# Mixture of experts on one core: weighted expert rows summed in DRAM by ordered, accumulating scatters

## The reference

```python
xn = layernorm(x)
x = x + segment_sum(edge_weight[:, None] * xn[dst], src, 6250) + attention(xn)   # a linear-cost attention, 8 heads
z = layernorm(x)
logits = z @ gate_w + gate_b                     # 16 experts
v, idx = top_k(logits, 2);  w = softmax(v)       # two experts per token
h = relu(z @ w1[e] + b1[e]);  o_e = h @ w2[e] + b2[e]      # 256 -> 512 -> 256, only for e in idx
y = z + sum_k w[k] * o_idx[k]
out = x + (layernorm(y) * gamma + beta)
```

## Time and profile before

| | us |
|---|---|
| median of 3 runs | 2754.63 (2744.38 to 2778.39) |
| the profiled execution | 2739.31 |
| its span, first to last instruction | 2737.4 |
| before the gate | 0 to 1913.2 |
| gate and table | 1913.2 to 2120.7 |
| expert tiles | 2120.7 to 2560.2 |
| combine | 2560.2 to 2737.4 |

### The profile page before, as it was taken

The page is one execution under the profiler, slowest core; times in us unless marked ns, Lnnn a source line. Parts: engine busy times, 40 slices in busy tenths (PEclk is TensorE's granted clock), DMA queues, the critical chain, the costliest instruction groups (busy, mean ns, idle before and its releaser), DMA issues.

```text
span 2737.4 us, 43467 instructions
## 1 busy us (share of the span) xinstructions
PE 2028.5 (74%) x12138; PEld 1334.9 (49%) x12139; DVE 1622.2 (59%) x4163; ACT 819.7 (30%) x2169; POOL 1294.0 (47%) x1239
## 2 busy tenths in 40 slices
PE   4656766888888887888888888888552999999400
PEld 3434543455444453444444444444552999999300
DVE  6888888888888885444444445444444233233377
ACT  4645631111111111222222222222321444444332
POOL 1263343777777775565655566553454000000375
PEclk9768978999999998998989898988555999999755
DMA  5300010222222222232322222247822333333343
GB/s 168 119 31 27 24 28 28 83 81 81 79 80 81 81 82 64 83 89 81 89 77 83 84 89 86 84 76 65 296 73 98 99 106 106 104 105 108 100 120 119
DMA packets 147105, 243.46 MB, mean 89 GB/s; under 512 B 27874, under 2 KB 104932, under 8 KB 146949
## 3 DMA queue, kind: packets, MB, share of 16 engines
q0 software_dynamic: 55488, 149.11, 20.2%
q1 hardware_dynamic: 88500, 89.91, 10.2%
q10 hardware_dynamic: 2960, 2.55, 0.3%
HBM read 190.08 MB, written 51.38 MB: 88 GB/s over the span
## 4 chain that ended last, share of the span: by engine, by line
PE 36%; another core or an unknown queue 7%; issue 6%; DVE 5%; POOL 3%; DMA 2%; ACT 1%; DVEq 1%; SPq 1%; ACTq 0%; POOLq 0%
PE bank L1956 8%; PE b L1716 7%; PE bqk L1976 7%; PE bank L1833 4%; PE bqk L1844 3%; PE b L1728 2%; POOL big L741 2%; DMA big<-xn_dram,big 2%; POOL big L710 1%; PE bank L1916 1%; DVE big L1466 1%; DVE acc L1259 1%; ACT mid L896 1%; DVE big L1249 1%
## 5 line engine op out<-in xcount | busy, mean ns | idle before, releaser
L710 POOL DMA_INDIRECT big<-xn_dram,big x880 | 916.1, 1041 | 529.4 <-issue 201.4
L1716 PE MATMUL b<-big 128*128 128x256 f32 x1760 | 538.4, 434 | 96.8 <-DVE acc L1259 46.2
L1716 PEld LDWEIGHTS b<-big 128*128 128x128 f32 x1760 | 338.1, 210 | 340.2 <-issue 179.8
L1259 DVE TENSOR_TENSOR acc<-acc,b 128x256 f32 x440 | 183.9, 418 | 366.6 <-remote 195.0
L741 POOL DMA_INDIRECT big<-y_dram,idxz x100 | 112.3, 1123 | 491.6 <-issue 484.0
L1249 DVE TENSOR_SCALAR big<-big 128x128 f32<-128x128 f32 x880 | 300.5, 363 | 7.8 <-DVE big L1299 7.7
L879 ACT ACTIVATE big<-bank 128x512 f32<-128x512 f32 (+1 forms) x208 | 105.4, 576 | 501.9 <-PE bank L1833 276.9
L1956 PEld LDWEIGHTS bank<-late,mid 128*128 128x128 f32 x1872 | 228.6, 193 | 7.6 <-DVE mid L1583 1.7
L1956 PE MATMUL bank<-late,mid 128*128 128x128 f32 x1872 | 229.2, 276 | 1.5 <-DVE mid L1583 1.5
L1976 PE MATMUL bqk<-big,mid 128*128 x928 | 219.5, 379 | 0.0
L1592 DVE TENSOR_TENSOR mid<-bqk,mid 128x256 f32<-128x256 f32 x116 | 49.3, 425 | 246.4 <-PE bqk L1976 246.4
(11 more groups left out here) (322 smaller groups left out, 3186.3 us busy)
## 6 DMA issues: line engine op xcount, KB each, us to landing
big<-w SPq DMA_DIRECT2D x8, 2048.0 KB
mid<-z_dram SPq DMA_DIRECT2D x120, 128.0 KB, 2.1
mid<-b SPq DMA_DIRECT2D x118, 128.0 KB, 3.0
y_dram<-mid SPq DMA_DIRECT2D x116, 128.0 KB, 1.7
big<-xn_dram,big POOLq DMA_INDIRECT x880
acc<-x_pad SPq DMA_DIRECT2D x10, 640.0 KB, 6.4
xn_dram<-big SPq DMA_DIRECT2D x10, 640.0 KB
y_out<-big SPq DMA_DIRECT2D x10, 640.0 KB
```

The lines of the kernel that those rows point to most:

```text
L710: pool.indirect_dma_start(out=gx[t % EB], out_offset=None, in_=xn_dram, in_offset=bass.IndirectOffsetOnAxis(ap=dstA[:, t:t + 1], axis=0)). ...
L1259: v.tensor_tensor(mine, mine, ps_pair[p % 2][:, 0:C], ALU.add).then_inc(s_add, 1)
L1716: a = pe.matmul(ps_pair[p % 2][:, 0:C], wd[t % (2 * EB)], gx[t % EB], start=(j == 0), stop=(j == 1))
```

## The change

The experts' results no longer go to y_dram to be gathered by token. There is a table sum_dram with one row per token. In the gate, SP stores z of each unit there. z's scattered rows are four elements wider (ZW = 260): the token's number, its first expert, the difference of its two softmax weights and the lower weight. So the row itself says where its result belongs and how it is weighted. For each expert tile DVE reads these columns (meta), adds the bias; ACT multiplies the rows by their weights (weigh); POOL scatters them with addition onto sum_dram, each scatter awaiting the one before. The combine loads plain rows, which hold z plus both weighted results. z tiles have two buffers instead of four, results four instead of two. Gate and combine loops are written out (static addresses) where they were loops of the engines. POOL adds beta to acc during the expert tiles and multiplies by gamma in the combine.

SP:

```diff
-            for a in range(0, 20, U):
-                sp.dma_start(z_dram[X * R + a * P:X * R + (a + U) * P, :].rearrange("(p r) c -> p (r c)", p=P),
-                             zero).then_inc(s_zz, 16)
+            sp.dma_start(sum_dram[NP:NP + P, :], zero[:, 0:C]).then_inc(s_zz, 16)
+            sp.dma_start(beta_b[:], beta.partition_broadcast(P)).then_inc(s_gb, 16)
...
             for e in range(0, X, 4):
                 sp.dma_start(w2s[:, e:e + 4], w2[e:e + 4].rearrange("e (c p) f -> p e c f", p=P)).then_inc(s_w, 16)
+            for u in range(NU):
+                sp.wait_ge(s_z, (u + 1) * U)
+                sp.dma_start(sum_dram[u * U * P:(u + 1) * U * P, :].rearrange("(u p) c -> p u c", p=P),
+                             zt5[u % 2][:, :, 0:C]).then_inc(s_zst[u % 2], 16)
+            sp.wait_ge(s_dz, 4)
+            sp.dma_start(z_dram[X * R:, :].rearrange("(r p) c -> p r c", p=P),
+                         padrow.unsqueeze(1).broadcast_to([P, 20, ZW])).then_inc(s_pz, 16)
...
             with sp.Fori(0, FT // 4) as i:
                 for k in range(4):
                     t = 4 * i + k
                     sp.wait_ge(f_zT, t + 1)
-                    load_z(t + 4, k)
+                    sp.wait_ge(f_meta, t + 1)
+                    load_z(t + 2, k % 2)
                     sp.wait_ge(f_yo, t + 3)
-                    sp.dma_start(y_dram[ds(t * P, P), :], yo[k % 2]).then_inc(s_yst[k % 2], 16)
                     load_b2(t + 2, k % 2)
...
+            for u in range(NU):
+                sp.dma_start(zc[u], sum_dram[u * U * P:(u + 1) * U * P, :].rearrange("(u p) c -> p u c", p=P)).then_inc(s_zl[u // 2], 16)
```

POOL:

```diff
+            for t in range(FT):
+                pool.wait_ge(f_ys, t + 1)
+                if t:
+                    pool.wait_ge(s_ysc[(t - 1) % 4], 16 * ((t - 1) // 4 + 1))
+                pool.indirect_dma_start(out=sum_dram, in_=yo[t % 4], in_offset=None,
+                                        out_offset=bass.IndirectOffsetOnAxis(ap=idxy[t % 4][:, 0:1], axis=0),
+                                        compute_op=ALU.add).then_inc(s_ysc[t % 4], 16)
+                if 4 <= t < 4 + NT:
+                    mine = acc[:, t - 4, :]
+                    pool.tensor_tensor(mine, mine, beta_b[:], ALU.add).then_inc(s_xb, 1)
+            pool.wait_ge(s_gb, 32)
+            for u in range(NU):
+                pool.wait_ge(s_fn, u + 1)
+                pool.tensor_tensor(zc[u], zc[u], gamma_b.unsqueeze(1).broadcast_to([P, U, C]), ALU.mult).then_inc(s_gm, 1)
```

ACT:

```diff
+            def gate_z(u):
+                k = u % 2
+                act.wait_ge(s_gsc, u + 1)
+                if u >= 2:
+                    act.wait_ge(s_zst[k], 16 * (u // 2))
                 for j in range(U):
                     t = u * U + j
+                    if u >= 2:
+                        act.wait_ge(s_zsc[k][j], 32 * (u // 2))
+                    act.activation(zt5[k][:, j, 0:C], acc[:, t, :], ACT.Identity, scale=rstd[:, t:t + 1], bias=nbias[:, t:t + 1]
+                                   ).then_inc(s_z, 1)
+
+            def gate_exp(u):
+                act.wait_ge(s_df, u + 1)
+                act.activation(ew[:], df[:], ACT.Exp).then_inc(s_ew, 1)
...
+            for u in range(NU):
+                gate_root(u)
+                gate_z(u)
+                if u:
+                    gate_exp(u - 1)
+                gate_turn(u)
+            gate_exp(NU - 1)
...
+            def weigh(t, k):
+                act.wait_ge(f_yo, t + 3)
+                act.wait_ge(f_meta, t + 1)
+                act.activation(yo[k], yo[k], ACT.Copy, scale=wslot[k][:]).then_inc(f_ys, 1)
...
+            with act.Fori(1, FT // 4) as i:
                 for k in range(4):
                     t = 4 * i + k
+                    expert(t, k)
+                    weigh(t - 1, (k - 1) % 4)
```

DVE (gate_back, behind the experts' choice; expert_four; combine):

```diff
+                if u < NU - 1:
+                    scales(u + 1, s_grt, s_gsc)
+                if u >= 2:
+                    for j in range(U):
+                        v.wait_ge(s_zsc[k][j], 32 * (u // 2))
+                join()
+                mark(v.tensor_copy(zt5[k][:, :, C], idcol[:]))
+                mark(v.tensor_copy(zt5[k][:, :, C + 1], idf[:, :, 0]))
+                v.wait_ge(s_ew, u + 1)
+                link(v.tensor_scalar(wsum[:], ew[:], 1.0, None, ALU.add))
+                link(v.reciprocal(wsum[:], wsum[:]))
+                link(v.tensor_tensor(wlow[:], ew[:], wsum[:], ALU.mult))
+                mark(v.tensor_tensor(zt5[k][:, :, C + 2], wsum[:], wlow[:], ALU.subtract))
+                mark(v.tensor_copy(zt5[k][:, :, C + 3], wlow[:]))
                 v.wait_ge(s_rk, u + 1)
...
+            def meta(t, k, i):
+
+                v.wait_ge(s_ztin[k % 2], 32 * i + 16 * (k // 2 + 1))
+                if not (isinstance(i, int) and i == 0):
+                    v.wait_ge(s_ysc[k], 16 * i)
+                mark(v.tensor_copy(idxy[k][:], zt[k % 2][:, C:C + 1]))
+                link(v.scalar_tensor_tensor(out=wmask[:], in0=zt[k % 2][:, C + 1:C + 2], scalar=etau[:, ds(t, 1)],
+                                            in1=zt[k % 2][:, C + 2:C + 3], op0=ALU.is_equal, op1=ALU.mult))
+                link(v.tensor_tensor(wslot[k][:], wmask[:], zt[k % 2][:, C + 3:C + 4], ALU.add))
+                v.sem_inc(f_meta, 1)
+
             def expert_four(i, first):
                 for k in range(4):
                     t = 4 * i + k
+                    meta(t, k, i)
                     v.wait_ge(f_y, t + 1)
                     v.wait_ge(s_b2in[k % 2], 32 * i + 16 * (k // 2 + 1))
-                    if not (first and k < 2):
-                        v.wait_ge(s_yst[k % 2], 32 * i + 16 * (k // 2))
-                    v.tensor_tensor(yo[k % 2], ps_y2[k % 2], b2t[k % 2], ALU.add).then_inc(f_yo, 1)
+                    v.tensor_tensor(yo[k], ps_y2[k % 2], b2t[k % 2], ALU.add).then_inc(f_yo, 1)
                     copy_w(t + 3, k + 1)
...
+            for u in range(NU + 2):
+                if u < NU:
+                    combine_front(u)
+                if u >= 2:
+                    combine_out(u - 2)
+                if u < NU:
+                    scales(u, s_crt, s_csc)
```

PE:

```diff
                     hidden(t + 1, k + 1)
-                    pe.wait_ge(s_ztin[(k + 2) % 4], 16 * (i + 1 + (k + 2) // 4))
+                    pe.wait_ge(s_ztin[k % 2], 32 * i + 16 * (k // 2 + 2))
                     turn_z(t + 2, k + 2)
```

More of the change, by code:

```diff
@@ L66 @@
 R = NP + P
+ZW = C + 4
 FT = 116
@@ L735, in _ @@
[L735 to L743 removed]
+            pool.wait_ge(s_gb, 16)
@@ L921, in evac_zT, with expert @@
                 act.activation(zT[k % 2], ps_zT[k % 2].rearrange("p (c n) -> p c n", c=2), ACT.Copy).then_inc(f_zTe, 1)
+            def weigh(t, k):
+                act.wait_ge(f_yo, t + 3)
+                act.wait_ge(f_meta, t + 1)
+                act.activation(yo[k], yo[k], ACT.Copy, scale=wslot[k][:]).then_inc(f_ys, 1)
+            def expert(t, k):
+                ex = act.value_load(expI[0:1, ds(t, 1)], min_val=0, max_val=X - 1)
+                act.wait_ge(f_hT, t + 1)
+                for c in range(FC):
+                    a = act.activation(hT[k % 2][:, c, :], ps_hT[k % 2][:, c * P:(c + 1) * P], ACT.Relu,
+                                       bias=b1c[:, ds(ex * FC + c, 1)])
+                a.then_inc(f_hTe, 1)
+                evac_zT(t + 2, k)
@@ L1406, in query_half, with scales, gate_back @@
                                        op0=ALU.add, op1=ALU.mult).then_inc(s_o, 1)
+            def scales(u, root, done_):
+                cols = slice(u * U, (u + 1) * U)
+                v.wait_ge(root, u + 1)
+                link(v.reciprocal(rstd[:, cols], std5[:]))
+                v.scalar_tensor_tensor(out=nbias[:, cols], in0=mv[:, cols, 0:1].rearrange("p u o -> p (u o)"), scalar=-1.0,
+                                       in1=rstd[:, cols], op0=ALU.mult, op1=ALU.mult).then_inc(done_, 1)
             def gate_front(u):
-                row_stats(lambda j: tile(u * U + j), mv[:, ds(u * U, U), :])
-                v.sem_inc(s_ask, 1)
-            def gate_back(u, k, i, first, more):
+                row_stats(lambda j: tile(u * U + j), mv[:, u * U:(u + 1) * U, :])
+                v.sem_inc(s_gst, 1)
+            def gate_back(u):
+                k = u % 2
                 v.wait_ge(s_lg, u + 1)
@@ L1536, in _ @@
             gate_front(0)
-            unit_scales(0, NU + NK)
-            gate_pair(0, True)
-            loop(1, NU // 2 - 1, gate_pair)
-            gate_pair(NU // 2 - 1, False)
+            scales(0, s_grt, s_gsc)
+            for u in range(NU):
+                if u < NU - 1:
+                    gate_front(u + 1)
+                gate_back(u)
             join()
@@ L1933, in _ @@
             logits(0, 0)
[L1934 to L1940 removed]
+            for u in range(NU):
+                rank(u)
+                if u < NU - 1:
+                    logits(u + 1, (u + 1) % 2)
             pe.wait_ge(s_cc, NU + 1)
```

364 lines of the change are left out of this document (132 added, 232 removed).

## The result

The changed kernel takes 3380.33 us (median of 4 runs, 3366.61 to 3398.78) where the kernel before takes 2762.4 (median of 4, 2744.38 to 2778.39): 1.224 times as long (95% interval 1.214 to 1.235). The forecast was 3290, in a range of 3070 to 3460.

| stage | before | after | difference | predicted |
|---|---|---|---|---|
| before the gate | 1913.2 | 1941.9 | +28.7 | 0 |
| gate and table | 207.5 | 234.9 | +27.4 | +30 |
| expert tiles | 439.5 | 1116.9 | +677.4 | +611 |
| combine | 177.2 | 88.7 | -88.5 | -97 |

What follows compares the result with a forecast made beforehand. Before the change, TensorE bounds the expert stage, POOL and DVE the combine. 2739.3 + 611 (expert tiles) + 30 (gate) - 97 (combine) = 3283; the runs' median lies 15 us higher, so 3290, range 3070 to 3460.

Steps and rivals of the forecast that it cites:

- closed chain: Expert tiles: with two z buffers and the wait for meta, these steps run serially once per tile, 8.0 us at full clock.
- The size, 9.0 us: Expert tiles: time per tile with the clock alternating, 116 x 9.0 = 1044 us, +611; chance 0.62.
- 8.0 at full clock: Expert tiles: sum of the serial steps per tile; as a rival with the clock always full, 3167 us, chance 0.10.
- The level to alternate, with the second layer mostly on the low one: Expert tiles: TensorE's clock switches between full and half, the second layer following the gap: 9.0 us a tile.
- the row with 3.00 busy of 3: Profile row of the kernel before, cited as the unbroken TensorE work that brought the clock back to 0.99.
- rival 2: Expert tiles: the clock stays low all through, 9.8 us a tile, +704, total 3376 us; chance 0.14.
- Below 9.0 it is hidden: Expert tiles: the ordered scatters, 3.1 to 5.6 us each, are covered by the z load's chain.
- The price, 4.4: Expert tiles: time per ordered accumulating scatter in us, taken in the middle of 3.1 to 5.6.
- only the scatters' order is new: 4.4 us a tile: Rival for the expert tiles: z load stays hidden, +78, total 2750 us (2889 at 5.6 a tile); chance 0.05.
- The gate, +30: Gate: a late initial sum store and units that no longer overlap, 20.1 us a unit; bounds 0 to +45.
- The +44 by the drain: Gate: the skill's drain would cost each of ten exps 1.4 us more; weighed, but the measured duration was used.
- The combine, -97: Combine: gathers and multiply-adds removed, plain sum loads added, 77 to 80 us instead of 177; bounds -110 to -80.

Runs made afterwards that it cites:

- the chain opened (and no scatters): Changed kernel with meta two tiles ahead on DVE, SP's order shifted by two tiles, and its 116 expert scatters removed: 2734.12 us.
- the filler run: Changed kernel with 28 more transposes per tile on TensorE into an unused bank, ahead of the wait for z: 3218.0 us.
- the opened chain: Changed kernel with meta two tiles ahead on DVE and SP's order shifted by two tiles, scatters still adding: 2932.5 us, 1.061 times the kernel before.
- the kernel before with the serial load: Kernel before, its z load of tile t+2 waiting for a DVE one-column copy behind the weight copy: 3503.22 us against 2763.67 on the same chip.
- the last chip: Chip of the changed kernel with the combine's gamma product on DVE instead of POOL: 3192.51 us, where the kernel before took 2551.95.

## Why the prediction was right

- **"Second layer(t-1), bias add, weight copy, meta, load, transposes, second layer(t) is a closed chain."** Shown: without scatters the tile stays, with the chain alone the kernel before gets slow, and with the chain opened (and no scatters) a tile is back at 3.94.
- **The size, 9.0 us.** Measured 9.57, 66 us over the stage. Three terms were off. Meta is 0.40, not 0.75. From the transposes' start to the second layer it is 1.00, not 0.55: the prediction says that the register load stands behind the transposes, and yet counts one of the two. They take 0.44 and 0.53 (the 0.44 at full clock too: it is the same in the filler run). And the second layer took 3.45 up to the bias add, not the 3.1 that remains in a tile of 9.0. The first error went the other way than the last two, so the sum is better than its terms: 8.0 at full clock, where the filler run has 8.24.
- **Slips in its arithmetic.** 8.0 with 1.73 more is 9.7, not 9.8, and the long values of the chain's terms add up to 10.4, not 10.2. Neither moves the result out of the range.
- **The clock.** "The level to alternate, with the second layer mostly on the low one": its link has a minimum of 2.03, a median of 3.57 and a maximum of 3.82. That it comes from the clock is shown by the filler. One second layer, from its first matmul at 2391.45, in two windows (the granted clock is the third number from the right):

```profile
2391.40:2392.40 1.00, 0.95 (x4) 0.87 (x5) 0.00 (x0) 0.97 (x4) 0.39 (x1) 1.00 0.00 0
2392.40:2394.70 2.30, 2.30 (x8) 1.92 (x7) 0.33 (x1) 0.51 (x2) 1.92 (x2) 0.50 0.28 17
```

  It begins at full clock and falls to 1.2 GHz within its first microsecond. By the rule of the Trainium skill ("TensorE: Matmul & The Clock Gate", section "HAM oscillation — how this bites in real kernels") every tile would start cold; the trace agrees for 63 of 116 second layers; in the other 53 the clock is full at the first matmul. One ground of the prediction was misread: the row with 3.00 busy of 3 has the clock back already (0.99). What stands ahead of the rise, in the kernel before, is the row that the earlier trace rows leaves out:

```profile
1849.00:1855.00 6.00, 5.26 (x20) 1.46 (x20) 1.76 (x5) 0.00 (x0) 3.77 (x4) 0.50 0.75 72
```

- **Luck in the total.** 3380 is nearer to rival 2 (clock low throughout, 3376) than to the forecast of 3290. That is no sign for the rival: its tile of 9.8 is longer than the 9.57 measured, and the 28.7 us ahead of the gate, which no sum had, make up for it. With 3.82 in every tile the measured links would give 9.9. The clock, 0.77 and alternating, decides for the forecast.
- **The scatters beside it.** "Below 9.0 it is hidden", and it is. The price, 4.4, "in the middle", is close to the 3.8 and 0.73 of a scatter with no weight copy beside it, and too low for what the opened chain has: 5.74 a tile, just above the high bound of 5.6. The bound was a gather's landing added to a plain scatter; the addition also takes POOL 0.6 to 0.8 us longer (medians), which no row had shown. The rival "only the scatters' order is new: 4.4 us a tile" was the right second limit; it would have been 2932, not 2750. The addition of beta was taken at 0.6 us, a fifth of a large one; it takes 1.28, in the shadow.
- **The gate, +30.** Measured +27.4, by the two mechanisms named: the first wait for the sum's store (predicted to about 1970, one wait of 29.1) and the units that no longer overlap (103.6 us of waits for the exp): they follow each other at 19.4 us, where the sum has 20.1, with 17 table loads where it has ten pairs. The +44 by the drain that the Trainium skill ("ScalarE: Activation LUTs", section "What ACT_TABLE_LOAD costs") puts beside a table load was rightly left out. The trace has no such gap; the load starts 0.02 us behind the row before it, and the exp 0.01 behind the load:

```profile
2017.72 0.60 ACT L927 ACTIVATE mid<-acc,nbias,rstd 128x256 f32<-128x256 f32 x1 [1.76 <-DMA z_dram<-mid,idxz]
2018.34 1.28 ACT L932 ACT_TABLE_LOAD   x1
2019.63 0.21 ACT L932 ACTIVATE ew<-df 128x5 f32<-128x5 f32 x1
```

- **The combine, -97.** Measured -88.5: "ACT and POOL's gamma product keep up" failed, because the product (3.76 on average, not 3.07) and DVE exclude each other. With the product on DVE it is 77.1.
- **Not seen.** SP's queue holds the z load by the b2 load's wait as well as by f_meta. The prediction had f_meta alone; moving only that is worth 0.33 us a tile.
- **Open.** The 28.7 us ahead of the gate. The code there is the same but for a few semaphores, and in the other kernels on changed code the gate began anywhere from 1924 to 1954 (1767 on the last chip); the kernel before with the serial load had 1932. No run separates change from spread. Of the 101 us between the sum of the terms (3283) and the profiled execution (3384.1), 66 are the tile, 29 this, 9 the combine, and the gate gave 3 back.

## What to carry to other kernels

When an engine's queue gets a wait on something that a later stage makes, write out every queue that it passes, and look for a cycle through all of them: here three (DVE, SP, TensorE) closed a loop of 9.6 us around 3.73 us of work, and opening one of them gave almost nothing. Before buffers are saved or a second pass is replaced by an accumulating transfer, price that transfer back to back, not spaced: the 88 us won in the combine were less than the 209 that ordered additions cost with the loop open (in the order in which that kernel had DVE's weight copy beside them). An engine "in the shadow" can still hold another one by a shared port, so read the duration of short instructions beside its long ones.

## What the runs showed of the hardware

- An indirect DMA with addition (128 rows of 1 KB) takes POOL 1.55 us and lands after 3.8 us in the changed kernel, a plain one 0.96 and 2.4. With meta and SP's queue ahead the medians are 1.78 and 5.3, and the long landings go with DVE's 128x1024 copy running undisturbed beside the scatter (16 of 18 against 2 of 32). That the copy is the cause is argued from the trace alone.
- What a sequencer does early while its engine is busy is paid in full behind a wait: TensorE's register load cost nothing in the kernel before (2300.40 to 2300.62 from transposes to second layer) and leaves a gap of 0.53 us in each tile after the change. SP needs 0.96 from meta's end to its issue. DVE's 0.5 ahead of the weight copy was there before.
- More matmuls can shorten a stage that waits: 3248 additional ones took 155 us off the expert tiles (964.4 us from the first z load, where the changed kernel has 1119.2), by a clock of 0.99 instead of 0.77.
- POOL's 128x1280 product and a DVE instruction with two inputs in SBUF exclude each other: 0.17 us became 2.62, and 2.87 became 4.14.
